# An expert feed-forward kernel on one Trainium2 core: the three passes of the second expert product issued ahead of those of the first, in every round

## What is computed

```
x = x + 0.5 * ffn(layernorm(x))
x = x + attn(layernorm(x))          # dilated, cheap
x = x + 0.5 * ffn(layernorm(x))

def ffn(x):
    x = conv(x) + conv_b
    q, k, v = split(x @ wqkv.T + bqkv)          # 16 heads of 8
    x = layernorm(x + softmax(q k / sqrt(8)) v @ wo.T + bo) * ln1_g + ln1_b
    probs = softmax(x @ gate_w + gate_b)        # 8 experts
    h = relu(einsum('bsd,edf->bsef', x, w1) + b1)        # the first expert product, 512 wide
    y = einsum('bsef,efd->bsed', h, w2) + b2             # the second expert product
    return layernorm(x + einsum('bse,bsed->bsd', probs, y)) * ln2_g + ln2_b
```

## Time and profile before

| | us |
|---|---|
| median of three runs | 1595.32 |
| lowest and highest | 1593.14, 1599.85 |
| the profiled execution | 1598.26 |
| its span, first to last instruction | 1596.5 |
| TensorE busy in it | 1511.8 |
| VectorE, ScalarE, GpSimd busy | 1166.5, 1129.4, 1025.5 |

### The profile page before, as it was taken

The page is one execution under the profiler, slowest core; times in us unless marked ns, Lnnn a source line. Parts: engine busy times, 40 slices in busy tenths (PEclk is TensorE's granted clock), DMA queues, the critical chain, the costliest instruction groups (busy, mean ns, idle before and its releaser), DMA issues.

```text
span 1596.5 us, 26004 instructions
## 1 busy us (share of the span) xinstructions
PE 1511.8 (95%) x8226; PEld 825.7 (52%) x8226; DVE 1166.5 (73%) x1831; ACT 1129.4 (71%) x1652; POOL 1025.5 (64%) x979
## 2 busy tenths in 40 slices
PE   3798999999999999999999999999999999999986
PEld 2233555555555555555555555555555555554565
DVE  2767677777777777877778787687777777767475
ACT  2466777777777767777776777677777777777775
POOL 3421667777676767768687776777767676767143
PEclk9968999999999999999999999999999999999999
DMA  6533334151432425243332523425233331511010
GB/s 175 134 93 86 90 81 101 41 147 48 113 82 72 102 62 140 48 117 85 88 93 54 151 57 79 102 56 139 53 101 86 94 96 43 145 41 48 27 48 27
DMA packets 88014, 137.40 MB, mean 86 GB/s; under 512 B 11013, under 2 KB 51894, under 8 KB 83254
## 3 DMA queue, kind: packets, MB, share of 16 engines
q1 hardware_dynamic: 86598, 131.53, 32.3%
q0 software_dynamic: 1280, 4.20, 1.0%
HBM read 102.66 MB, written 32.77 MB: 85 GB/s over the span
## 4 chain that ended last, share of the span: by engine, by line
PE 77%; DVE 9%; issue 4%; DMA 4%; POOL 2%; ACT 2%; SPq 1%; DVEq 0%; POOLq 0%; ACTq 0%
PE hid_y L997 15%; PE ctx_ps L1167 13%; PE hid_y L1001 12%; PE hid_y L998 12%; PE score L1035 10%; DVE negmax L865 2%; DMA m_xn<-out 2%; PE misc L997 2%; PE misc L1001 1%; PE misc L998 1%; PE score L1055 1%; PE misc L1109 1%; DMA f_xn<-in_L_attn_x 1%; DVE ctxT L872 1%; POOL e_ve L553 1%
## 5 line engine op out<-in xcount | busy, mean ns | idle before, releaser
L865 DVE TENSOR_REDUCE negmax<-score 128x2 f32<-128x1024 f32 x484 | 590.4, 1220 | 228.0 <-PE score L1035 227.9
L590 POOL TENSOR_TENSOR hidl<-hid,hidh 128x512 fp32r<-128x512 f32 x456 | 586.0, 1297 | 247.6 <-DVE hidh L824 121.3
L706 ACT ACTIVATE probs<-score 128x1024 f32<-128x1024 f32 x468 | 480.0, 1026 | 117.7 <-PE score L1055 117.7
L735 ACT ACTIVATE hid<-hid_y,cols 128x512 f32<-128x512 f32 x484 | 331.5, 685 | 173.6 <-PE hid_y L1001 165.7
L1167 PE MATMUL ctx_ps<-probs,V 128*18 128x512 f32 x2048 | 278.8, 617 | 10.3 <-DVE ctxT L872 10.3
L1055 PE MATMUL score<-Qp,Kp 32*128 32x512 f32 (+1 forms) x1024 | 270.0, 508 | 2.3 <-ACT probs L699 2.0
L1035 PE MATMUL score<-Kp,Qp 24*128 24x512 f32 x968 | 246.1, 502 | 23.0 <-DVE negmax L865 12.0
L997 PE MATMUL hid_y<-x1h,w1h 128*128 128x512 f32 x484 | 235.5, 487 | 1.5 <-DVE negmax L865 1.3
L598 POOL TENSOR_TENSOR yacc<-yacc,gated 128x512 f32<-128x512 f32 x128 | 171.6, 1341 | 66.1 <-DVE gated L840 66.1
L997 PE MATMUL hid_y<-hidh,w2h 128*128 128x512 f32 x512 | 208.0, 406 | 4.7 <-DVE gated L840 4.7
L1001 PE MATMUL hid_y<-hidl,w2h 128*128 128x512 f32 x512 | 203.5, 397 | 0.0
(11 more groups left out here) (182 smaller groups left out, 1792.5 us busy)
## 6 DMA issues: line engine op xcount, KB each, us to landing
gate_b<-gate_dram SPq DMA_DIRECT2D x128, 256.0 KB, 3.7
q_parts_dram<-q_parts SPq DMA_DIRECT2D x48, 256.0 KB, 3.0
k_parts_dram<-k_parts SPq DMA_DIRECT2D x48, 256.0 KB, 3.0
Qp<-q_parts_dram SPq DMA_DIRECT2D x64, 192.0 KB
Kp<-k_parts_dram SPq DMA_DIRECT2D x64, 192.0 KB
Qp<-q_parts_dram SPq DMA_DIRECT2D x32, 240.0 KB
Kp<-k_parts_dram SPq DMA_DIRECT2D x32, 240.0 KB
Qp<-q_parts_dram SPq DMA_DIRECT2D x32, 144.0 KB
```

Source lines behind the costliest of these rows:

```text
L590: pool.tensor_tensor(hidl[:, n % RING, :], hid[:, n % 2, :], hidh[:, n % RING, :].bitcast(F32), ALU.subtract).then_inc(s["h_lo"], 1)
L706: act.activation(probs[:, n % 2, 2 * j:2 * j + 2, :], score2[:], ACT.Exp, scale=SCALE)\
L735: act.activation(hid[:, n % 2, :], hid_bank(u, n), ACT.Relu, bias=col(n))\
L865: dve.tensor_reduce(negmax[:, g % 2, :, k % 8], banks_for_max(u.count(32, k))[:], AX.X, ALU.max, negate=True).then_inc(s["a_max"], 1)
```

## The change

The block that issues D (`m = T - EXPERTS_AT - DOWN_LAG`) is moved ahead of the block that issues H (`m = T - EXPERTS_AT`). Each block keeps its waits, its operands and its semaphores. Only TensorE's queue differs; those of the other four engines are the same instruction for instruction.

```diff
--- before.py
+++ after.py
@@ -1170,21 +1170,6 @@
                                          stop=(place == 1 and kc == TC - 1))
                     last.then_inc(s["a_pv"], 1)
 
-                m = T - EXPERTS_AT
-                if 0 <= m < 64 and m % 2 == 0:
-                    n = m // 2
-                    if n == 0:
-                        wait(pe, s["c_x1h"], u.count(1, 1))
-                        wait(pe, s["a_max"], EARLY_MAX)
-                    if i0 < 2:
-                        wait(pe, s["set_wl"], E)
-
-                    if alone(u, n) and not alone(u, n - 1):
-                        wait(pe, s["a_max"], 32 * UNITS)
-                    wait(pe, s["h_full"], u.count(32, n - 1 if alone(u, n - 1) else n))
-                    w = slice(n * 128, (n + 1) * 128)
-                    three(hid_bank(u, n), w1h[:, w], w1l[:, w], x1h[:], x1l[:],
-                          before_rlo=(s["c_x1l"], u.count(1, 1)) if n == 0 else None).then_inc(s["h_mm"], 1)
                 m = T - EXPERTS_AT - DOWN_LAG
                 if 0 <= m < 64 and m % 2 == 0:
                     n = m // 2
@@ -1196,6 +1181,21 @@
                             wait(pe, s["set_wl"], 2 * E)
                     three(y_ps, w2h[:, n, :], w2l[:, n, :], hidh[:, n % RING, :], hidl[:, n % RING, :],
                           start=(f == 0), stop=(f == FC - 1)).then_inc(s["y_mm"], 1)
+                m = T - EXPERTS_AT
+                if 0 <= m < 64 and m % 2 == 0:
+                    n = m // 2
+                    if n == 0:
+                        wait(pe, s["c_x1h"], u.count(1, 1))
+                        wait(pe, s["a_max"], EARLY_MAX)
+                    if i0 < 2:
+                        wait(pe, s["set_wl"], E)
+
+                    if alone(u, n) and not alone(u, n - 1):
+                        wait(pe, s["a_max"], 32 * UNITS)
+                    wait(pe, s["h_full"], u.count(32, n - 1 if alone(u, n - 1) else n))
+                    w = slice(n * 128, (n + 1) * 128)
+                    three(hid_bank(u, n), w1h[:, w], w1l[:, w], x1h[:], x1l[:],
+                          before_rlo=(s["c_x1l"], u.count(1, 1)) if n == 0 else None).then_inc(s["h_mm"], 1)
 
             def mid(T, b, t, i, i0):
                 if T == AT["m_xT"]:
```

More of the change, by code:

```diff
@@ L1171, in tick @@
                     last.then_inc(s["a_pv"], 1)
+                m = T - EXPERTS_AT - DOWN_LAG
+                if 0 <= m < 64 and m % 2 == 0:
+                    n = m // 2
+                    e, f = divmod(n, FC)
+                    wait_lo(pe, u, n + 1)
+                    if f == 0:
+                        wait(pe, s["y_gated"], u.count(8, e))
+                        if i0 < 2:
+                            wait(pe, s["set_wl"], 2 * E)
+                    three(y_ps, w2h[:, n, :], w2l[:, n, :], hidh[:, n % RING, :], hidl[:, n % RING, :],
+                          start=(f == 0), stop=(f == FC - 1)).then_inc(s["y_mm"], 1)
                 m = T - EXPERTS_AT
@@ L1187, in tick @@
                           before_rlo=(s["c_x1l"], u.count(1, 1)) if n == 0 else None).then_inc(s["h_mm"], 1)
-                m = T - EXPERTS_AT - DOWN_LAG
-                if 0 <= m < 64 and m % 2 == 0:
-                    n = m // 2
[L1191 to L1194, removed]
-                        if i0 < 2:
-                            wait(pe, s["set_wl"], 2 * E)
-                    three(y_ps, w2h[:, n, :], w2l[:, n, :], hidh[:, n % RING, :], hidl[:, n % RING, :],
-                          start=(f == 0), stop=(f == FC - 1)).then_inc(s["y_mm"], 1)
             def mid(T, b, t, i, i0):
```

## The result

The changed kernel takes 1627.86 us (median of four runs, 1621.21 to 1635.3) beside 1594.23 us for the kernel before (four runs, 1591.9 to 1599.85). The ratio is 1.0207, with a 95% interval of 1.0154 to 1.026: slower by about 33 us, where 15 were forecast. The profiled execution took 1626.59 us with a span of 1624.8, so it is 28.3 us longer than the one before (1596.5).

What follows compares the result with a forecast made beforehand. TensorE was taken as the bound, issuing almost without a gap. The terms, 6.2 + 7.3 - 3.1 + 1.7 + 3.5 - 0.7, gave +14.9 us on the 1595.3 us median: 1610 us, range 1598 to 1619.

Steps and rivals of the forecast that it cites:

- term E: Expert rounds without scores, ends of units 14 and 15: period stays, last H slips behind the waiting D28; +3.5 us.
- The first part of E: End of unit 14: last H slips behind waiting D28, delaying x1h, L715 and L1125 of unit 15; +1.6 us.
- The second part: End of unit 15: last H stands behind the waiting D28, so D31 comes later; +1.9 us.
- A: Unit starts: later last H delays x1h and L715, so gate matmul L1125 starts 0.44 us late in 14 units; +6.2 us.
- B: Fifth D of a unit (D4) must wait for VectorE's gated, 0.52 us late in 14 units; +7.3 us.
- rival of nothing to be seen: The hole before the context product swallows the unit-start delay, 3 to 7 us remain, about 1600 us; chance 0.21.
- Term C: Six units: later holes, scores waiting for row maxima behind a DMA-timed statistics step, absorb the D4 delay; -3.1 us.
- term D: Unit 14 after the last row maximum: ScalarE's exponentials come later and scores wait in five rounds; +1.7 us.
- F: Unit 14: D5 runs while H8 waits for the last row maximum, a gain; -0.7 us.
- The clock rival: Pairs of holes in each of 14 units bring TensorE's clock down, +23 us, 1633 us; chance 0.08 (over 1619).

Runs made afterwards that it cites:

- `gated` ahead of the subtraction: The changed kernel with VectorE's `gated` issued ahead of the `hidl` subtraction in the rounds without row maxima; 1614.29 us, ratio 1.0101.
- the repeat: The changed kernel measured and profiled once more, nothing altered; 1622.24 us, ratio 1.0174 to the kernel before.
- the tail alone: The kernel before, with D first only in the rounds without row maxima, from H 8 of unit 14 on; 1608.82 us, ratio 1.0070.
- the three undone: The changed kernel with H first again in the rounds of H 7 and H 31 and those without row maxima; 1596.16 us, ratio 0.9998.
- D first where it gains: The kernel before, with D first in every fourth tail round and at H 8 of unit 14, `gated` ahead of the subtraction there; 1596.19 us, ratio 1.0012.
- the tail put back: The changed kernel with H first again in the rounds without row maxima, from H 8 of unit 14 on; 1605.23 us, ratio 1.0052.
- H 7 first: The changed kernel with H first again in the round of H 7 of every unit; 1616.39 us, ratio 1.0123.
- the last H first: The changed kernel with H first again in the round of each unit that holds H 31; 1607.77 us, ratio 1.0084.

## Why the prediction was wrong

**The step that failed is term E**, in its words "Both orders have that H there, so the period stays". It was true of TensorE and was checked on TensorE alone. `gated` is on VectorE, and what stands ahead of it there is the subtraction for the H of the round before. With H first, three products (D, H, D) lay between the end of that H and the end of the D that `gated` reads, 2.1 us at 0.70 each. With D first only one lies between, 0.69 us (1597.41 to 1598.10). Between the end of an H and the end of its subtraction pass the two evictions and the subtraction itself, about 2.1 us (1597.41 to 1599.5). The cover before was therefore zero, and all of the shift counted: 1.31 us per period, in unit 15 and in the last rounds of unit 14. The row that would have told this, the subtraction that ends 0.01 us ahead of `gated` with ScalarE as its own releaser, stands directly above the row at 1580.49 on VectorE, which the prediction used. The prediction had named the cause, H's last pass ending 0.71 us later, and said that everything that waits for H had been looked at; it had not followed the subtraction to what queues behind it. The forecast for the tail was +4.5 us and the traces have 17.9 and 16.6.

The first part of E was too small as well, 2.4 instead of 1.6. From D 28 to D 31 of unit 14 both the changed kernel and the one with `gated` ahead of the subtraction are 1.9 us longer than before, 0.3 more than forecast; from there to D 4 of unit 15 the changed kernel is 0.5 us longer and the other 0.9 shorter, so that the first part is 0.95 in the latter. The excess is thus again `gated` behind the subtraction. The second part was right, 2.0 against 1.9: D 31 starts 3.82 us after D 28 (2.25 before, about 4.1 expected), it waits for its own `hidl`, and the rest is behind it:

```profile
1611.53 0.50 PE L997 MATMUL hid_y<-hidh,w2h 128*128 128x512 f32 x1 [0.79 <-DVE hidl L830]
```

**Terms A and B were right.** L1125 starts 0.06 us behind L715, D 4 is 0.52 us late. Together they should cost 0.96 us per unit, and the distance of neighbouring units grew by 1.0. The experiments gave each back alone (about 0.5 and 0.5) and both together (0.0 left). The rival of nothing to be seen fell on the place it named itself: the hole in front of the context product stayed at 0.73 us, so A was not swallowed.

**Term C had the right sign and, as far as these profiles can tell, the right size, but it is not a number that one profile can give.** The scores' wait behind the DMA-timed statistics step varies from one profile to the next, even with the same order of instructions. VectorE's wait in that step, in the kernel before, the changed one and its repeat:

```profile
DVE m_st L809 <- DMA m_xn<-out: 13.3, 8, 2.9
```

```profile
DVE m_st L809 <- DMA m_xn<-out: 5.4, 6, 2.4
```

```profile
DVE m_st L809 <- DMA m_xn<-out: 2.8, 5, 1.4
```

From H 0 of unit 0 to D 4 of unit 14 the four profiles in which neither A nor B is at work (before, the tail alone, the three undone, D first where it gains) have 1320.7, 1316.3, 1319.0 and 1317.3 us, mean 1318.3. The four with both (the changed kernel twice, the tail put back, `gated` ahead) have 1327.2, 1324.9, 1328.8 and 1332.7, mean 1328.4. The difference is 10.1 us, where A + B - C was 10.4; with four profiles a side, which scatter over 4 and 8 us, it is good to about 2 us (an estimate from that scatter). Some of the scatter is a stretch of half clock outside unit 14, which stands in the kernel before (1019.3), in the three undone (636.6) and in `gated` ahead (645.8). TensorE's wait for row maxima is 10.4 us on average in the first four and 6.7 in the others, 3.7 less, where C was 3.1. The two profiles of the changed kernel alone would have said 4.2 and 6.4.

**Terms D and F had the right size, but the table's rows do not measure them.** F is seen in its wait. The first H without a row maximum beside it waited 1.31 us and now waits 0.42, in both profiles of the changed kernel:

```profile
1489.25 0.50 PE L997 MATMUL hid_y<-x1h,w1h 128*128 128x512 f32 x1 [0.42 <-DVE negmax L865]
```

The kernel with D first where it should gain differs from the one with the three undone, from D 4 to D 8 of unit 14, in the rounds of this H and of H 10 alone (and in the place of `gated`), and that stretch takes 10.78 us instead of 11.48: the 0.7 of the forecast. Of term D, five scores and one context product of unit 14 wait for exponentials, 1.6 us in all. This is the line of the five:

```profile
PE score L1055 <- ACT probs L706: 1.3, 5, 0.3
```

Three of the six stand ahead of D 12, in the row named after F. With `gated` ahead of the subtraction, D 8 to D 20 is 1.8 us longer than before, where the forecast was 1.7. In the changed kernel D 12 to D 20 alone is 1.8 longer, but 0.6 of that is `gated` again (1.1 with `gated` ahead): that this row agrees with the forecast is luck. The row D 4 to D 12 is crossed by the stretch of half clock as well, which stands at 1473.3 in the kernel before, at 1484.3 in the first profile of the changed one and nowhere in the repeat, so neither +0.8 nor -0.6 is a measure of F.

**The clock rival was wrong for the units and right in one place.** After the pairs of holes there is no new stretch at half clock in units 1 to 14. In the first profile the clock is whole from 157 us to 1484 (the line at 1019 below is a part of that), and one stretch stands in unit 14, as in the earlier trace rows; the repeat has the same three holes in front of that place (0.86, 0.70 and 0.46 us) and no stretch. So what the prediction cited from the Trainium skill (TensorE: Matmul & The Clock Gate, A second HAM failure mode: psum-queue depth-cycling) did not come about where it could have cost 23 us. What did cost something, once in the tail, is a single long hole. The hole in front of D 4 of unit 15 grew from 1.59 us to 2.77, and behind it the granted clock was 0.50 (1.2 GHz, the lower level). The row at D 4, then stretches (us, busy TensorE, its loads, VectorE, ScalarE, GpSimd, granted clock) in unit 14, at 1019, and behind D 4 of unit 15:

```profile
1561.96 0.47 PE L997 MATMUL hid_y<-hidh,w2h 128*128 128x512 f32 x1 [2.77 <-DVE gated L840]
```

```profile
1484.30:1487.60 3.30, 3.15 (x10) 2.11 (x10) 1.13 (x1) 0.22 (x1) 2.93 (x3) 0.50 0.53 161
1019.00:1022.30 3.30, 3.30 (x21) 1.76 (x24) 1.69 (x4) 2.15 (x3) 2.63 (x5) 1.00 0.91 259
```

```profile
1562.80:1566.10 3.30, 3.30 (x9) 2.58 (x8) 0.48 (x2) 1.26 (x2) 2.41 (x2) 0.50 0.30 88
1566.10:1600.00 33.90, 26.49 (x110) 19.97 (x108) 15.82 (x24) 23.95 (x38) 7.14 (x4) 1.00 0.16 38
```

The first period of unit 15 (D 4 to D 8) grew by 2.86 us instead of 1.31, so this stretch cost about 1.55 us. The repeat has the same (2.79 us of hole, a clock of 0.52 behind it). The kernel with the tail put back, where the hole is 1.60 us, does not have it.

**The whole.** With the mean of the middle (10.1), the tail (16.6 to 17.9) and nothing for the start-up, the change costs 27 to 28 us, inside the intervals of both measurements (24.6 to 41.5 us and 21.9 to 33.7). The +33 us of the first median are not explained beyond that; the repeat gave +27. The parts measured alone, +8 and +11 us, add to less than the whole, 19 us. Their intervals (4 to 12 and 8 to 14 us) leave room for 26, and the tail alone had in its profile a middle 4.5 us shorter than the kernel before's. What these holes depend on from run to run was not settled.

## What to carry to other kernels

When a product moves later, follow it two steps: to the instruction on the other engine that consumes it, and to whatever stands behind that consumer on its in-order queue; an instruction whose own inputs are early can be late through its neighbour. Before saying that a period stays, read for its waiting instruction the row directly above on its own engine: if that row ends within a few hundredths of a us of its start and waits itself for what is moved, there is no cover. And put a price on moves around irregular, DMA-timed holes only from several profiles, or from units in which no such hole stands.

## What the runs showed of the hardware

The start-up differs from one profile to the next by up to 10 us, more than any single term of the forecast. Up to the first H all kernels here have the same instructions in the same order on TensorE, yet that H started at 147.4 us in one profile and at 157.4 in another. In the page's row of the granted clock (40 slices of the span, tenths), the changed kernel and the one with the tail put back differ in the first slices:

```profile
PEclk7567999999999999999999999999999999999998
```

```profile
PEclk9978999999999999999999999999999999999999
```

So a comparison of two profiles should begin behind the start-up.

Holes of 0.5 to 0.8 us on TensorE in units 1 to 13 left the clock at its upper level in both profiles of the changed kernel, while the one of 2.8 us at D 4 of unit 15 had 3.3 us at the lower level behind it in both; nine matmuls ran in that time. Where that hole was 2.3 us long (`gated` ahead) about the same was lost, 1.45 us; where it was 1.9 us (H 7 first) the clock stayed whole behind it. The stretches inside the units fit this: they begin within 1.5 us behind a hole of 2.12 us in the kernel before, of 2.26 with `gated` ahead, and of 2.25 with the three undone. The kernel with the last H first has a hole of 2.06 us, at 832.08, and no stretch behind it. The stretch in unit 14 does not fit: three holes of under 1 us stand ahead of it, and with the same holes it comes in some profiles and not in others.
